# Relative-bias attention: the biased scores return to their PSUM bank, and ScalarE reads them there

## The chip, the cores and the metric

The kernel runs on one core of a Trainium2 chip. The metric is the device time of one execution in microseconds (us). TensorE multiplies and transposes (PE in the profile, its weight loads PEld), VectorE (DVE) and ScalarE (ACT) work element by element, GpSimd (POOL) does a little of the same, and SyncE (SP) issues the DMAs. Each engine runs its own instructions in order; between engines the program synchronises by semaphores, `wait_ge` and `then_inc`.

## The reference

The program computes a sequence model of four layers, each an attention-like part and a feed-forward part, on 8 sequences of 512 tokens and 128 features. Only the attention of the second layer (L1) is touched. In the reference:

```
q = shape(hidden_states @ Wq)          # H = 16 heads of DK = 64
k = shape(hidden_states @ Wk)
v = shape(hidden_states @ Wv)
scores = jnp.einsum('bhqd,bhkd->bhqk', q, k)
position_bias = compute_bias(s, s, rel_bias_table)   # depends on key - query only
scores = scores + position_bias
attn = jax.nn.softmax(scores, axis=-1)
out = jnp.einsum('bhqk,bhkd->bhqd', attn, v)
out = jnp.transpose(out, (0, 2, 1, 3)).reshape(b, s, H * DK)
return out @ Wo
```

So for every sequence and head a 512 x 512 matrix of scores gets a bias, a softmax along its rows, and is multiplied with the values. All of it is float32.

## The kernel before

The sequences pass one after the other through the same chain of stages. A hardware loop (`Fori`) takes the first six, and two more copies of the code, with the prefixes y and z in the tile names, take the last two; the stage therefore runs 8 times. The stage in question is `attn1`. It stands between the mixture-of-experts stage `moe` and the stage `lora1`, with nothing else beside it: all engines leave one stage before the next begins.

**Units and slots.** In the stage the work is cut into 64 units. A unit is 128 query rows of one head against all 512 keys, a tile of 128 x 512. Two heads go together (a head pair, eight units: four row blocks j, and in each the heads a = 0 and 1). All engines run through the same numbered slots, s = 0, 1, 2, ..., one unit a slot, each with its own lag written into the code. The letters below are those that the prediction uses for the steps of unit u:

- **S**: TensorE computes the scores of units s and s+1, two matmuls (line 2043), at every even slot s. They go to PSUM banks s % 4 and (s+1) % 4: `NS_ = 4` banks go round. From slot 4 on S has to wait until its two banks are free.
- **R**: VectorE adds the bias to the scores, takes the row's negated maximum `nmax`, and writes the sum to the SBUF tile `biased` (line 2145, one `tensor_tensor_reduce`; `maxed` counts it). Its slot is the unit's own.
- **E**: ScalarE takes exp(biased - max) into `prob`, with the row's sum in `den` (line 2116, followed by an instruction that reads the accumulator; `exped` counts it). It stands at slot u + 2 in ScalarE's order (`EXP = 2`).
- **V**: VectorE takes the reciprocal of `den` and scales `prob` by it (lines 2150 and 2152, `scaled`), at slot u + 1 of its own order, after R of unit u + 1.
- **T**: TensorE transposes the unit's `prob` (line 2050) at slot u + 4 (`TURN = 4`), into one of two banks that the ring of T and M shares, PS[4] and PS[7].
- **C**: ScalarE copies the transposed tile to `probt` (line 2124), also at slot u + 4, after that slot's E. It frees the ring's bank (`freed`).
- **W**: TensorE multiplies transposed probabilities and values (line 2064), at odd slots, for the head pair before.
- **M**: TensorE makes q, k and the values of the next head pair (lines 2014 and 2018), at slots 0, 2 and 4 of eight, between T of the even slot and T of the odd one. ScalarE moves each to SBUF (lines 2098 and 2095), after C of that even slot. At slot 4 of eight ScalarE also empties the product bank PS[5] (line 2105), and at slot 6 TensorE projects instead of making (line 2025).

So TensorE's order from an even slot s on is S(s, s+1), T(s-4), M, T(s-3), W. ScalarE's is E(s-2), C(s-4), the move of M, E(s-1), C(s-3). At the start of the stage C, T and W have nothing to do yet: TensorE's order is S(0,1), M, S(2,3), M, S(4,5), T(0), M, T(1), S(6,7), T(2), T(3), S(8,9), ..., with the first W at slot 13.

Of the kernel before, what the change touches and what calls it, by code (L numbers as in the profile page):

```python
# [19 lines left out]
ACT = mybir.ActivationFunctionType  # L20
# [4 lines left out]
P = 128  # L25
D = 128
SEQ = 512
NJ = SEQ // P
BIG = 3.0e38
# [42 lines left out]
def bass_mk_seq(nc, x, cols_f, cols_b, ends, wf, wb, lora, lora_cols, onehot, table, w2, out):  # L72
# [31 lines left out]
    PS = [BANKS[:, i, :] for i in range(8)]  # L104
# [1725 lines left out]
    def layers(b, scan_next, pre_next):  # L1830
# [113 lines left out]
        with Stage("attn1") as st:  # L1944
            def await_weights(sp):
# [14 lines left out]
            NS_, NP_, NT_ = 4, 6, 2 * PAIR  # L1960
# [1 line left out]
            qk = st.sb("qk", [P, 2, 2, SEQ])  # L1962
            vals = st.sb("vals", [P, 2, NJ, 2 * DK])
            toep = st.sb("toep", [P, 4, TW])
            biased = st.sb("biased", [P, NS_, SEQ])
            prob = st.sb("prob", [P, NP_, SEQ])
            probt = st.sb("probt", [P, NT_, SEQ])
            nmax, den, rden = (st.sb(n, [P, U]) for n in ("nmax", "den", "rden"))
            ot = st.sb("ot", [P, 2, SEQ])
            toep_ld = [st.sem(f"toep_ld{i}") for i in range(4)]  # L1970
            filled, freed, scored, maxed, exped, inverted, scaled = (
                st.sem(n) for n in ("filled", "freed", "scored", "maxed", "exped", "inverted", "scaled"))
# [21 lines left out]
            with nc.Block() as block:  # L1994
# [10 lines left out]
                def _(pe):  # L2005
# [26 lines left out]
                    for s in range(LAST):  # L2032
                        r, at = s // PAIR, s % PAIR
                        if s < U and s % 2 == 0:
                            j = unit(s)[1]
                            if at == 0:
                                pe.wait_ge(freed, place["make", r, 1] + 1)
                            if s >= NS_:
                                pe.wait_ge(maxed, s - NS_ + 2)
                            for a in range(2):  # L2040
                                o = DK * a
                                q, k = qk[o:o + DK, r % 2, 0, :], qk[o:o + DK, r % 2, 1, :]
                                nc.tensor.matmul(PS[(s + a) % NS_], q[:, j * P:(j + 1) * P], k,
                                                 start=True, stop=True).then_inc(scored, 1)
                        u = s - TURN
                        if 0 <= u < U:
                            pe.wait_ge(scaled, u + 1)
                            bank = ring(place["turn", u])
                            for kt in range(NJ):
                                last = nc.tensor.transpose(bank[:, kt * P:(kt + 1) * P],  # L2050
                                                           prob[:, u % NP_, kt * P:(kt + 1) * P], ident)
                            last.then_inc(filled, 1)
                        kt = WEIGH_AT.get(at)
                        w = r - (2 if at < TURN else 1)
                        if kt is not None and 0 <= w < NPAIR:
                            if kt == 0:
                                pe.wait_ge(freed, place["turn", PAIR * w + PAIR - 1] + 1)
                                pe.wait_ge(freed, place["make", w, 2] + 1)
                                if w:
                                    pe.wait_ge(emptied, w)  # L2060
                            for a in range(2):

                                first = PAIR * (w % 2) + a
                                last = nc.tensor.matmul(PS[5][DK * a:DK * (a + 1), :],
                                                        vals[:, w % 2, kt, DK * a:DK * (a + 1)],
                                                        probt[:, first:first + PAIR - 1:2, kt * P:(kt + 1) * P],
                                                        start=(kt == 0), stop=(kt == NJ - 1), skip_group_check=True)
                            if kt == NJ - 1:
                                last.then_inc(weighed, 1)
                        p = r - 2  # L2070
                        if at == PROJECT_AT and 0 <= p < NPAIR:
                            project(p)
                        if made_in(s):
                            make(*made_in(s))
# [11 lines left out]
                @block.scalar  # L2086
                def _(act):
                    def move(r, i):
                        n = place["make", r, i]
                        act.wait_ge(filled, n + 1)  # L2090
                        bank = RING[n % 2]
                        if i == 2:
                            if r >= 2:
                                act.wait_ge(weighed, r - 1)
                            nc.scalar.copy(vals[:, r % 2, :, :], bank.rearrange("p (j v) -> p j v", j=NJ)).then_inc(freed, 1)
                        else:
                            dst = qk[:, r % 2, i, :].rearrange("p (j t) -> p j t", j=NJ)
                            nc.scalar.copy(dst if i else dst[:, :, ::-1],
                                           bank.rearrange("p (j t) -> p j t", j=NJ)).then_inc(freed, 1)

                    def empty(w):
                        act.wait_ge(weighed, w + 1)
                        if w >= 2:
                            act.wait_ge(projected, w - 1)
                        nc.scalar.copy(ot[:, w % 2, :].rearrange("p (j t) -> p j t", j=NJ)[:, :, ::-1],
                                       PS[5].rearrange("p (j t) -> p j t", j=NJ)).then_inc(emptied, 1)

                    move(0, 0)
                    move(0, 1)
                    for s in range(LAST):  # L2110
                        e = s - EXP
                        if 0 <= e < U:
                            act.wait_ge(maxed, e + 1)
                            if e >= NP_:
                                act.wait_ge(filled, place["turn", e - NP_] + 1)
                            nc.scalar.activation(prob[:, e % NP_, :], biased[:, e % NS_, :], ACT.Exp, bias=nmax[:, e:e + 1],  # L2116
                                                 scale=-1.0, accum_out=den[:, e:e + 1]).then_inc(exped, 1)
                        u = s - TURN
                        if 0 <= u < U:
                            n = place["turn", u]  # L2120
                            act.wait_ge(filled, n + 1)
                            if u >= NT_:
                                act.wait_ge(weighed, (u - NT_) // PAIR + 1)
                            nc.scalar.copy(probt[:, u % NT_, :], RING[n % 2]).then_inc(freed, 1)  # L2124
                        w = s // PAIR - 2
                        if s % PAIR == EMPTY_AT and 0 <= w < NPAIR:
                            empty(w)
                        if made_in(s):
                            move(*made_in(s))
                    empty(NPAIR - 1)  # L2130

                @block.vector
                def _(dve):
                    V = nc.vector
                    for s in range(U + 1):
                        if s < U:
                            r, j, a = unit(s)
                            h = 2 * r + a
                            if j == 0:
                                dve.wait_ge(toep_ld[h % 4], 16 * (h // 4 + 1))  # L2140
                            dve.wait_ge(scored, s + 1)
                            if s >= NS_:
                                dve.wait_ge(exped, s - NS_ + 1)
                            c = P * (NJ - 1 - j)
                            V.tensor_tensor_reduce(biased[:, s % NS_, :], PS[s % NS_], toep[:, h % 4, c:c + SEQ], -1.0, BIG,  # L2145
                                                   ALU.add, ALU.min, nmax[:, s:s + 1]).then_inc(maxed, 1)
                        u = s - 1
                        if u >= 0:
                            dve.wait_ge(exped, u + 1)
                            V.reciprocal(rden[:, u:u + 1], den[:, u:u + 1]).then_inc(inverted, 1)  # L2150
                            dve.wait_ge(inverted, u + 1)
                            V.tensor_scalar(prob[:, u % NP_, :], prob[:, u % NP_, :], rden[:, u:u + 1], None,  # L2152
                                            ALU.mult).then_inc(scaled, 1)
                    dve.wait_ge(projected, NPAIR)
                    V.tensor_tensor(X[:, :, :], X[:, :, :], PS[6].rearrange(tiles, j=NJ), ALU.add)
# [211 lines left out]
```

## Time and profile before

| what | value |
|---|---|
| median of 3 runs | 5668.21 us (5660.7 to 5670.02) |
| the profiled execution | 5647.6 us, of which the span of the instructions is 5645.7 us |
| TensorE busy | 4758.2 us, 84% of the span |
| VectorE busy | 3632.7 us, 64% |
| ScalarE busy | 2719.9 us, 48% |
| line 2145 (R, in the six loop passes) | 384 times, mean 684 ns |
| line 2116 (E, in the six loop passes) | 384 times, mean 730 ns |

The profile is of one execution, so durations are compared with its own 5645.7 us; the difference of 20.6 us between its 5647.6 us and the median is how executions differ. A line of the profile that groups instructions gives the line of the kernel, the engine, the operation, the tile written and the tiles read, the shapes, the count, the busy time, the mean duration, and the idle time of the engine before them with what ended it. A timeline gives start, duration and the same names. Times of matmuls overlap in it: the end of a matmul is later than the moment at which the next one may enter, so intervals on TensorE are best read from start to start.

### The profile page before, as it was taken

The numbers are of one execution on the slowest core, as the hardware profiler recorded it, in microseconds if no ns is written. First come the engines' busy times: TensorE is split into PE (matmuls) and PEld (weight loads), VectorE is DVE, ScalarE is ACT, GpSimd is POOL, SyncE is SP. The second block draws the span as 40 slices with busy tenths as digits, with TensorE's granted clock in tenths as the row PEclk, the third lists the DMA queues.
The fourth block names the chain that finished last, engine by engine and source line by source line (L and its number), as shares of the span: only waits on it lengthen the run. The fifth ranks groups of instructions, "written<-read, shape, count | busy, mean of one in ns | idle before, by whom it ended". The sixth has DMA issues, their size and how long they took to land. (4 is left out here: it accounts for less than half of the span.)

```text
span 5645.7 us, 70330 instructions
## 1 busy us (share of the span) xinstructions
PE 4758.2 (84%) x22340; PEld 2223.0 (39%) x22340; DVE 3632.7 (64%) x8308; ACT 2719.9 (48%) x5086; POOL 1504.1 (27%) x1900
## 2 busy tenths in 40 slices
PE   4688887988879888898888988889887988889888
PEld 2244244432444324443244432444334543344344
DVE  5766855677556785657755677655865668556545
ACT  2255553644536454364542654435554455436443
POOL 2612620136200451106401064010630116201100
PEclk8899998998989999999899998999988999989889
DMA  4411310123101231012200132001320113201000
GB/s 134 134 40 57 107 63 2 47 67 100 53 3 53 73 100 40 3 53 94 86 33 16 40 111 82 20 23 48 107 75 16 35 46 107 74 5 53 1 27 6
DMA packets 150414, 315.66 MB, mean 56 GB/s; under 512 B 16192, under 2 KB 24896, under 8 KB 150000
## 3 DMA queue, kind: packets, MB, share of 16 engines
q1 hardware_dynamic: 150016, 310.82, 17.3%
q8 instruction: 193, 3.16, 0.2%
q14 instruction: 205, 1.68, 0.1%
HBM read 307.55 MB, written 3.21 MB: 55 GB/s over the span
## 5 line engine op out<-in xcount | busy, mean ns | idle before, releaser
L195 PE MATMUL BANKS<-WB 128*128 128x512 bf16 x2080 | 580.7, 431 | 252.0 <-DVE heads_parts_q L1327 65.4
L757 POOL TENSOR_TENSOR heads_work<-heads_work,heads_c_all 128x512 f32<-128x512 f32 x384 | 493.0, 1286 | 468.7 <-DVE heads_work L791 463.5
L1497 ACT ACTIVATE heads_prob<-BANKS 128x512 f32<-128x512 f32 (+3 forms) x768 | 376.7, 517 | 254.8 <-PE BANKS L1394 248.8
L211 POOL TENSOR_TENSOR rstd<-rstd,WF 128x4 f32<-128x4 f32 x24 | 24.2, 1006 | 1663.0 <-DVE rstd L229 1663.0
L724 PE MATMUL BANKS<-heads_work,WF 128*128 128x512 f32 x768 | 444.0, 663 | 7.0 <-DVE m_du L767 7.0
L195 PEld LDWEIGHTS BANKS<-WB 128*128 128x128 bf16 x2080 | 216.0, 108 | 586.6 <-issue 253.2
L1538 DVE TENSOR_REDUCE heads_nmax<-BANKS 128x1 f32<-128x512 f32 x384 | 248.7, 681 | 66.4 <-PE BANKS L1394 65.8
L404 POOL TENSOR_TENSOR rstd<-rstd,WF 128x4 f32<-128x4 f32 x48 | 48.5, 1010 | 908.6 <-DVE rstd L425 908.6
L2145 DVE CUSTOM_DVE_ANT_0 attn_biased<-BANKS,attn_toep 128x512 f32<-128x512 f32 x384 | 262.8, 684 | 34.1 <-DMA attn_toep<-bias_line 21.0
L2124 ACT COPY attn_probt<-BANKS 128x512 f32<-128x512 f32 x384 | 223.5, 582 | 126.6 <-PE BANKS L2050 124.1
L2116 ACT ACTIVATE attn_prob<-attn_biased,attn_nmax 128x512 f32<-128x512 f32 x384 | 280.3, 730 | 1.1 <-DVE attn_nmax L2145 1.0
L1394 PE MATMUL BANKS<-heads_parts_kT,heads_parts_qT 64*128 64x512 bf16 (+3 forms) x768 | 238.6, 368 | 46.1 <-DVE heads_nmax L1538 28.4
L1535 DVE CUSTOM_DVE_ANT_0 BANKS<-BANKS,WF 128x384 f32<-128x384 f32 (+3 forms) x512 | 242.0, 503 | 48.7 <-PE BANKS L1394 45.9
L869 PEld LDWEIGHTS BANKS<-last_x_w,last_x_a 128*128 128x128 f32 x1536 | 208.0, 200 | 165.7 <-ACT last_x_a L909 84.9
L782 DVE TENSOR_TENSOR BANKS<-BANKS,m_du 128x512 f32<-128x512 f32 x256 | 179.0, 699 | 139.6 <-PE BANKS L716 139.4
L869 PE MATMUL BANKS<-last_x_w,last_x_a 128*128 128x128 f32 x1536 | 215.8, 286 | 61.2 <-ACT last_x_a L909 61.2
L791 DVE TENSOR_TENSOR_SCAN heads_work<-BANKS,heads_work 128x512 f32<-128x512 f32 x192 | 233.3, 1215 | 41.0 <-POOL heads_work L753 40.4
L753 POOL TENSOR_TENSOR heads_work<-heads_b_all,m_du 128x512 f32<-128x512 f32 x192 | 251.5, 1310 | 0.2 <-DMA heads_b_all<-bc_rows 0.2
L2050 PEld LDWEIGHTS BANKS<-WF,attn_prob 128*128 128x128 f32 x1536 | 163.8, 140 | 209.1 <-DVE attn_prob L2152 134.7
L2050 PE MATMUL BANKS<-WF,attn_prob 128*128 128x128 f32 x1536 | 240.3, 281 | 6.7 <-ACT attn_probt L2124 3.7
L741 ACT ACTIVATE BANKS<-m_delta,WF 128x512 f32<-128x512 f32 x256 | 177.6, 694 | 131.9 <-DVE s_work L791 87.1
L1394 PE MATMUL BANKS<-heads_qm,heads_parts_kT 64*128 64x512 bf16 (+3 forms) x768 | 215.1, 355 | 21.9 <-DVE heads_nmax L1538 18.0
(919 smaller groups left out, 10554.0 us busy)
## 6 DMA issues: line engine op xcount, KB each, us to landing
heads_c_all<-bc_rows SPq DMA_DIRECT2D x384, 256.0 KB, 3.2
heads_b_all<-bc_rows SPq DMA_DIRECT2D x192, 256.0 KB, 3.6
attn_toep<-bias_line SPq DMA_DIRECT2D x96, 448.0 KB, 4.4
last_x_w<-in_w SPq DMA_DIRECT2D x48, 512.0 KB, 3.5
s_c_all<-bc_rows SPq DMA_DIRECT2D x64, 256.0 KB, 3.3
yheads_c_all<-bc_rows SPq DMA_DIRECT2D x64, 256.0 KB, 3.2
s_b_all<-bc_rows SPq DMA_DIRECT2D x32, 256.0 KB, 3.7
yheads_b_all<-bc_rows SPq DMA_DIRECT2D x32, 256.0 KB, 3.6
```

Of the source, the lines that this page charges most:

```text
L195: nc.tensor.matmul(bank, ident_b, bc(ident_b[:, 0:1], [P, SEQ]), start=True, stop=True)
L724: nc.tensor.matmul(SUM, ident, work[:, m % RW, :], start=(n == 0), stop=(n == NS - 1)).then_inc(acc, 1)
L753: nc.gpsimd.tensor_tensor(work[:, s % RW, :], b_all[:, k % RB, :], du[:, d, t, :], ALU.mult).then_inc(drv[1], 1)
L757: nc.gpsimd.tensor_tensor(work[:, m % RW, :], work[:, m % RW, :], c_all[:, m % RC, :], ALU.mult).then_inc(rd, 1)
L869: last = nc.tensor.matmul(DOWN[e % 2][:, j * D:(j + 1) * D], a1[:, i % 3, j * P:(j + 1) * P], down_part(i), start=(t == 0 and j == 0), sto ...
L1394: nc.tensor.matmul(take(kind, i)[:, lo:hi], left[rows, P * tile:P * (tile + 1)], right[rows, lo:hi], start=True, stop=True).then_inc(sem, 1)
L1497: nc.scalar.activation(prob[:, i % PR, lo:hi], bank("T", i)[:, lo:hi], ACT.Exp).then_inc(exped, 1)
L1535: V.tensor_tensor_reduce(got, got, W("early")[:, SEQ - hi:], -1.0, BIG, ALU.add, ALU.min, nmax[:, j, h:h + 1]).then_inc(maxed, 1)
L1538: V.tensor_reduce(nmax[:, j, h:h + 1], got, AX.X, ALU.max, negate=True).then_inc(maxed, 1)
L2050: last = nc.tensor.transpose(bank[:, kt * P:(kt + 1) * P], prob[:, u % NP_, kt * P:(kt + 1) * P], ident)
L2116: nc.scalar.activation(prob[:, e % NP_, :], biased[:, e % NS_, :], ACT.Exp, bias=nmax[:, e:e + 1], scale=-1.0, accum_out=den[:, e:e + 1]). ...
L2145: V.tensor_tensor_reduce(biased[:, s % NS_, :], PS[s % NS_], toep[:, h % 4, c:c + SEQ], -1.0, BIG, ALU.add, ALU.min, nmax[:, s:s + 1]).the ...
```

## The change

VectorE's step R writes its sum back to the PSUM bank that it read, not to the SBUF tile `biased`, which is gone. ScalarE's step E reads that bank. The bank is free for the next scores when E is done, so TensorE's step S now waits for `exped` with the same number with which it waited for `maxed`: before S(s, s+1) the E of units s-4 and s-3 has to be over, where it was the R of these units. VectorE's wait for E of unit s-4, which kept R from overwriting `biased`, is taken out. No instruction is added, dropped or put at another place of its engine's order.

```diff
@@ -1962,7 +1962,6 @@
             toep = st.sb("toep", [P, 4, TW])
-            biased = st.sb("biased", [P, NS_, SEQ])
             prob = st.sb("prob", [P, NP_, SEQ])
@@ -2036,7 +2035,7 @@
                             if s >= NS_:
-                                pe.wait_ge(maxed, s - NS_ + 2)
+                                pe.wait_ge(exped, s - NS_ + 2)
                             for a in range(2):
@@ -2113,7 +2112,7 @@
-                            nc.scalar.activation(prob[:, e % NP_, :], biased[:, e % NS_, :], ACT.Exp, bias=nmax[:, e:e + 1],
+                            nc.scalar.activation(prob[:, e % NP_, :], PS[e % NS_], ACT.Exp, bias=nmax[:, e:e + 1],
                                                  scale=-1.0, accum_out=den[:, e:e + 1]).then_inc(exped, 1)
@@ -2139,10 +2138,8 @@
                             dve.wait_ge(scored, s + 1)
-                            if s >= NS_:
-                                dve.wait_ge(exped, s - NS_ + 1)
                             c = P * (NJ - 1 - j)
-                            V.tensor_tensor_reduce(biased[:, s % NS_, :], PS[s % NS_], toep[:, h % 4, c:c + SEQ], -1.0, BIG,
+                            V.tensor_tensor_reduce(PS[s % NS_], PS[s % NS_], toep[:, h % 4, c:c + SEQ], -1.0, BIG,
                                                    ALU.add, ALU.min, nmax[:, s:s + 1]).then_inc(maxed, 1)
```

## Rows read from the trace of the kernel before

**Rows 1.** Busy time by engine, one stretch (start:end, length, busy, PEclk, DMA):
```profile
353.00:480.00 127.00, 124.83 (x643) 59.73 (x641) 79.19 (x257) 97.54 (x224) 0.00 (x0) 1.00 0.18 59
```
**Rows 2.** Line 2116: count, ns min/median/max, first and last start, forms:
```profile
L2116 ACT ACTIVATE attn_prob<-attn_biased,attn_nmax x384: 721/726/751, 360.6 to 3905.9; 128x512 f32<-128x512 f32 x192
...
L2116 ACT ACTIVATE zattn_prob<-zattn_biased,zattn_nmax x64: 721/726/751, 5128.5 to 5244.6; 128x512 f32<-128x512 f32 x64
```
**Rows 3.** Timeline, one pair of slots in mid-stage (start, duration, instruction, [idle before]):
```profile
400.75 1.13 PE L2043 MATMUL BANKS<-attn_qk 64*128 64x512 f32 x4
...
401.25 0.68 DVE L2145 CUSTOM_DVE_ANT_0 attn_biased<-BANKS,attn_toep 128x512 f32<-128x512 f32 x1
...
401.81 0.66 PE L2050 MATMUL BANKS<-WF,attn_prob 128*128 128x128 f32 x4
...
402.31 1.02 PE L2014 MATMUL BANKS<-XT,WF 128*128 128x512 f32 x2
...
402.51 0.58 ACT L2124 COPY attn_probt<-BANKS 128x512 f32<-128x512 f32 x1 [0.71 <-PE BANKS L2050]
...
403.24 0.63 PE L2050 MATMUL BANKS<-WF,attn_prob 128*128 128x128 f32 x4
403.37 0.58 ACT L2098 COPY attn_qk<-BANKS 128x512 f32<-128x512 f32 x1 [0.28 <-PE BANKS L2014]
...
403.80 1.08 PE L2064 MATMUL BANKS<-attn_probt,attn_vals 128*64 128x512 f32 x4
403.85 0.72 ACT L2116 ACTIVATE attn_prob<-attn_biased,attn_nmax 128x512 f32<-128x512 f32 x1
```
**Rows 4.** Timeline, start of the stage:
```profile
355.85 0.59 ACT L2098 COPY attn_qk<-BANKS 128x512 f32<-128x512 f32 x1 [0.27 <-PE BANKS L2014]
...
356.49 1.13 PE L2043 MATMUL BANKS<-attn_qk 64*128 64x512 f32 x4 [0.68 <-ACT attn_qk L2098]
...
360.61 0.72 ACT L2116 ACTIVATE attn_prob<-attn_biased,attn_nmax 128x512 f32<-128x512 f32 x1
...
360.72 1.13 PE L2043 MATMUL BANKS<-attn_qk 64*128 64x512 f32 x4
361.24 0.19 ACT L2116 ACTIVATION_READ_ACCUMULATOR attn_prob<-attn_biased,attn_nmax 128x1 f32 x1
...
361.46 0.16 DVE L2150 RECIPROCAL attn_rden<-attn_den 128x1 f32<-128x1 f32 x1 [1.92 <-ACT attn_prob L2116]
...
361.80 0.72 ACT L2116 ACTIVATE attn_prob<-attn_biased,attn_nmax 128x512 f32<-128x512 f32 x1
...
362.20 0.66 PE L2050 MATMUL BANKS<-WF,attn_prob 128*128 128x128 f32 x4 [0.35 <-DVE attn_prob L2152]
```
**Rows 5.** Timeline of TensorE, S of slots 14 and 16:
```profile
377.47 1.13 PE L2043 MATMUL BANKS<-attn_qk 64*128 64x512 f32 x4
...
380.56 1.13 PE L2043 MATMUL BANKS<-attn_qk 64*128 64x512 f32 x4
```
**Rows 6.** Timeline, mid-stage, a slot where ScalarE also empties PS[5]:
```profile
407.04 0.59 ACT L2105 COPY attn_ot<-BANKS 128x512 f32<-128x512 f32 x1
...
407.99 0.74 ACT L2116 ACTIVATE attn_prob<-attn_biased,attn_nmax 128x512 f32<-128x512 f32 x1
...
408.86 1.13 PE L2043 MATMUL BANKS<-attn_qk 64*128 64x512 f32 x4
```
**Rows 7.** Groups by line and form (count | busy us, mean ns | idle before):
```profile
L1497 ACT ACTIVATE heads_prob<-BANKS 128x512 f32<-128x512 f32 x480 | 274.5, 596 | 174.2 <-PE BANKS L1394 170.9
...
L909 ACT ACTIVATE last_x_a<-BANKS,WF 128x512 f32<-128x512 f32 x192 | 128.9, 686 | 173.3 <-PE BANKS L881 172.2
...
L1535 DVE CUSTOM_DVE_ANT_0 BANKS<-BANKS,WF 128x512 f32<-128x512 f32 x16 | 10.8, 706 | 0.8 <-PE BANKS L1394 0.7
```
**Rows 8.** Timeline, start of the stage: C of unit 0, then T's weights:
```profile
363.50 0.56 ACT L2124 COPY attn_probt<-BANKS 128x512 f32<-128x512 f32 x1
...
364.18 0.42 PEld L2050 LDWEIGHTS BANKS<-WF,attn_prob 128*128 128x128 f32 x4 [0.63 <-issue]
```

## The prediction

> **What bounds the kernel now.** I read the page's busy shares first (TensorE 84%), but the change touches one stage only, so the next view is the busy time in that stage: of the 127 us from 353 to 480 TensorE works 124.83, ScalarE 97.54 and VectorE 79.19, at a granted clock of 1.00 [rows 1]. TensorE bounds it. The view of line 2116 gives the count: 384 and 64 exponentials, and 64 more in the y copy of the code, are 512 = 8 stages of 64 units [rows 2]. Whatever one stage loses or gains counts eight times, since nothing runs beside it.
>
> Then the timeline, to see what order the releases come in. In mid-stage TensorE never waits. Start to start, S takes 1.06 us (400.75 to 401.81), T 0.50, M 0.93, the second T 0.56 and W the rest [rows 3], and S comes back after 4.055 us on average (400.75 to 408.86 is two rounds) [rows 3, 6]. The bank that S waits for was released by R: the R that starts at 401.25 and takes 0.68 belongs to the banks of an S two rounds later, at 408.86, so that wait has over 6 us of room. This is the room that the change gives away.
>
> **The change part by part.**
>
> *E reads PSUM.* It takes 726 ns now, median, from SBUF with a bias per partition [rows 2]. No row shows exactly the new form. The nearest one is line 909, PSUM to SBUF, same shape, bias per partition: 686. The exponential of line 1497, also from PSUM, takes 596, but its bias is a constant [rows 7]. I take 686, 0.04 less than now, and keep 596 (0.13 less) and 726 (nothing less) as the ends. The Trainium skill (ScalarE: Activation LUTs, What ACT_TABLE_LOAD costs) says that each per-partition operand adds about 93 ns to an ACTIVATE. The gap between the two rows, 90 ns, agrees; going by 596 in spite of it would make the result 3.6 us a stage instead of 4.0. In mid-stage the 0.04 is worth nothing, because ScalarE waits for TensorE: C waits 0.71 for T and the move 0.28 for M [rows 3].
>
> *R writes PSUM.* Line 1535 is this instruction, in place in a bank: 706 against 680 [rows 3, 7]. VectorE's 79 of 127 us cover the 0.03, and R at 401.25 is over 1.9 us before the E that reads it at 403.85 [rows 1, 3]. Without that cover it would be 64 x 0.03 = 1.9 us a stage. I take 0, and the wait that is dropped on VectorE is worth 0 too, as R never came near it: it is for an E four units back.
>
> *S waits for E.* This is what counts. S(s, s+1) now needs E(s-3). The signal comes after the accumulator is read: E(0) starts at 360.61, its read ends at 361.43, and the reciprocal that needs it starts at 361.46 [rows 4]. So it is 0.82 after E's start, 0.78 with the shorter E. From ScalarE's signal to TensorE the row nearest in kind is S(0) itself: the copy ends at 356.44 and S starts at 356.49, 0.05 [rows 4]. A bank is released for S 0.83 us after the start of E. (Another such pair shows 0.12, from 364.06 to 364.18 [rows 8]; with that, and no shorter E, it would be 0.94.)
>
> Mid-stage, with M in the round, the new ring is: S, T after 1.06, M after 0.50, ScalarE's move 1.06 after M's start (402.31 to 403.37), E 0.48 later (403.37 to 403.85), release 0.83 later: 3.93 us [rows 3], against 4.055 of TensorE's own work. It does not bind, by 0.12. Where ScalarE also empties PS[5], E starts at 407.99 and S at 408.86, 0.87 later [rows 6], against 0.83 needed: room 0.04. Without M the ring is 1.06 + 0.70 (T to C) + 0.48 + 0.83 = 3.07, against 3.09 of TensorE's work (377.47 to 380.56) [rows 3, 5]. So in mid-stage all rings stay just inside.
>
> At the start they don't. There TensorE has less work in a round (no W before slot 13), and in the kernel before S used that to run ahead of E: S(4,5) starts at 360.72, beside E(0), before E(1) at 361.80 has begun [rows 4]. Now it needs E(1). Followed slot by slot, with E(1) 0.04 earlier:
> - S(4,5): 361.76 + 0.83 = 362.59, instead of 360.72 (+1.87). T(0), ready since 362.20 [rows 4], now stands in TensorE's order behind the waiting S and comes at 363.65, and with it M, C and the move.
> - S(6,7): this round has an M, 3.93: 366.52. S(8,9): no M, 3.07: 369.59. S(10,11): 3.93, 373.52. S(12,13): 3.93, 377.45. In each of these rounds TensorE's own work is 3.1 at most with M (4.055 less W's 1.0) and 2.1 without.
> - S(14,15): from slot 13 on W is there, so TensorE's 4.055 binds again, not 3.93: 381.50. S(16,17): 3.09: 384.59, instead of 380.56 [rows 5]: 4.03, of which I keep 4.0.
>
> From there on TensorE has the same back-to-back work as before, with no idle time in which the 4.0 us could be caught up. The sum is 8 x 4.0 = 32 us on the profiled span of 5645.7, or 0.57%. On the median of the runs shown, 5668.2, this gives 5700.
>
> The bounds with the release at other places: with E at 596 it is 0.09 earlier in five rings, 4.0 - 0.45 = 3.55 a stage, 28 us. With release at 0.94 the five first rings cost 0.55 more, the one at slot 16 another 0.09, the six emptying slots 0.07 each, and two late rounds without M 0.09 each: 5.2 a stage, 42 us.
>
> The Trainium skill (PSUM — Partial Sum Buffer, Summary: rules for kernel authors) has a rule that speaks against this change: evacuate promptly. Taken as a general price it would make every round longer; by the rows it has one only in the rounds up to slot 14. The mid-stage case is the second rival below.
>
> **The rivals.**
> 1. *The lead doesn't matter* (no measurable change, 5671). Before, TensorE also waited in the first slots, 0.35 us before T(0) for one [rows 4]. If only the first wait counted, and later idle time absorbed it, less than 0.4 us a stage would be left, 3 us. Against it: E comes after C and the move, these come after T and M, and T stands behind S. So the ring closes over every round, and does not dissolve after the first. 6%.
> 2. *The mid-stage binds as well* (5725). The rooms there are 0.12, 0.04 and 0.02. If the release is 0.17 later than I take it, because E reads a bank more slowly or the signal is slow, the rounds up to slot 16 cost 1.0 more, ten rounds with M 0.05 each, six emptying ones 0.13, two late ones 0.15: 4.0 + 2.6 = 6.6 a stage, 53 us; I call it 57 with a weight load that can no longer be ahead. For it: thin rooms. Against it: no slow read of a bank in the rows [rows 7]. 14%.
> 3. *The clock falls at the start* (5716). The first 20 us get some 4 us more idle time on TensorE. The granted clock is 1.00 over the stage now [rows 1]. If it went to its lower level once per stage, at 1.2 GHz, for the time of one ring, TensorE's part of that ring, 1.06 + 0.50 + about 0.4, would double: 2 us, 16 us in all. 10%. The Trainium skill (TensorE: Matmul & The Clock Gate, HAM oscillation) warns of waits that make the clock fall; no row of this stage shows it yet.
> 4. *Faster* (5655). ScalarE is the busy engine in the first slots. If S were never held, because E(s-3) is over by then, and E took 596, the first 12 units would each gain 0.13 there: 1.6 us a stage, 13 us. It decides from the point where E(1) ends before 360.72; by [rows 4] E(1) starts only at 361.80. 3%.
>
> **How the numbers follow.** The forecast, 5700, has 67%; its own range is 5691 to 5712, from 28 us and from 42 and with a few us of difference between executions. The rivals have 6, 14, 10 and 3%. Two times that differ by less than 0.2%, 11 us, can't be told apart here. Faster is rival 4, 3%. Within 0.2% are rival 1 and a little of the rest, 7%. Slower 90%. The range of 5685 to 5728 leaves out the cases with no loss and what is beyond the second rival.
>
> **What would show it.** In the profile after, S(4,5) starts about 6.1 us after S(0,1) (4.2 before) and after the second E has ended; idle time of TensorE before line 2042 (S) of about 1.9 us at first and 0.9 in the next rounds, ended by ScalarE's E; S(16,17) about 28.1 us after S(0,1), 24.07 before; E at 0.69 us, R at 0.71. From slot 16 on rounds of 4.05 us again. The forecast is wrong if those rounds are longer than 4.1 (then rival 2), if matmuls of the first slots get longer (rival 3), or if S(6,7) and later ones don't wait (rival 1).

## The result and the profile after

| | before | after |
|---|---|---|
| median | 5669.11 us (4 runs, 5660.7 to 5670.4) | 5708.52 us (4 runs, 5702.9 to 5719.5) |
| profiled span | 5645.7 us | 5717.5 us |
| one stage, S(0,1) to the last C | 123.04 to 123.06 us, all 8 | 127.25 us in 2, 128.87 us in 6 |
| the same, sum of 8 | 984.3 us | 1027.7 us |

The changed kernel is slower: ratio 1.0071, 95% interval 1.0057 to 1.0086, 39 us between the medians. The forecast was 5700, +32, with a range of 5685 to 5728. Under "stage" the table has the time from the start of S(0,1) to the end of the last C, in the profiled execution.

The lines are numbered anew in the changed kernel: S is line 2042, E 2115 and R 2142. First E in the six loop passes (count, ns min/median/max); then the groups of the first stage (count | busy us, mean ns | idle before), and for comparison S in the same stage of the kernel before:

```profile
L2115 ACT ACTIVATE attn_prob<-BANKS,attn_nmax x384: 687/695/732, 363.4 to 3952.9; 128x512 f32<-128x512 f32 x192
```
```profile
L2115 ACT ACTIVATE attn_prob<-BANKS,attn_nmax 128x512 f32<-128x512 f32 x64 | 45.0, 704 | 0.3 <-DVE attn_nmax L2142 0.3
L2142 DVE CUSTOM_DVE_ANT_0 BANKS<-BANKS,attn_toep 128x512 f32<-128x512 f32 x64 | 44.4, 694 | 5.7 <-PE BANKS L2042 5.3 <-DMA attn_toep<-bias_line 0.2
...
L2042 PE MATMUL BANKS<-attn_qk 64*128 64x512 f32 x128 | 37.1, 656 | 6.1 <-ACT attn_prob L2115 5.4 <-ACT attn_qk L2097 0.7
```
```profile
L2043 PE MATMUL BANKS<-attn_qk 64*128 64x512 f32 x128 | 36.1, 641 | 0.7 <-ACT attn_qk L2098 0.7
```

E takes 695 ns, median, where it took 726 [rows 2]; R takes 694, mean, where it took 684. These are close to the sizes expected (0.69 and 0.71 us). What the forecast left out is the instruction behind R that reads the accumulator: it takes 142 ns, mean, where it took 82, so R's step is 0.07 us longer in all. The line of S is the one to look for: TensorE stands idle before S, and E ends that idle time, 5.4 us in this stage. The kernel before had no such entry; its S had idle time before it only once, 0.7 us, until ScalarE had copied k.

The timeline of TensorE in the sixth pass shows the waits one by one. It is the answer to [rows 4] and [rows 5]; there S(4,5) came 4.23 us after S(0,1), and S(16,17) 24.07:

```profile
3828.45 1.13 PE L2042 MATMUL BANKS<-attn_qk 64*128 64x512 f32 x4 [0.68 <-ACT attn_qk L2097]
...
3834.56 1.13 PE L2042 MATMUL BANKS<-attn_qk 64*128 64x512 f32 x4 [1.81 <-ACT attn_prob L2115]
...
3838.52 1.13 PE L2042 MATMUL BANKS<-attn_qk 64*128 64x512 f32 x4 [0.86 <-ACT attn_prob L2115]
...
3841.68 1.13 PE L2042 MATMUL BANKS<-attn_qk 64*128 64x512 f32 x4 [1.01 <-ACT attn_prob L2115]
...
3845.62 1.13 PE L2042 MATMUL BANKS<-attn_qk 64*128 64x512 f32 x4 [0.82 <-ACT attn_prob L2115]
...
3849.55 1.13 PE L2042 MATMUL BANKS<-attn_qk 64*128 64x512 f32 x4 [0.82 <-ACT attn_prob L2115]
...
3853.61 1.13 PE L2042 MATMUL BANKS<-attn_qk 64*128 64x512 f32 x4
...
3856.77 1.13 PE L2042 MATMUL BANKS<-attn_qk 64*128 64x512 f32 x4
...
3860.82 1.13 PE L2042 MATMUL BANKS<-attn_qk 64*128 64x512 f32 x4
```

The S start 6.11, 10.07, 13.23, 17.17, 21.10, 25.16 and 28.32 us after the first. Five of them, S(4,5) to S(12,13), show idle time before them that E ended; from S(14,15) on none does. The round up to S(16,17) is 3.16 us, where TensorE's own work took 3.09 [rows 5], and behind it the rounds are 4.05 us again (3856.77 to 3860.82). S(16,17) is 28.32 - 24.07 = 4.25 us later than before, and the stage ends 4.2 us later. Nothing is caught up.

In six of the eight stages there is more. Here is the first of them, as TensorE's timeline and as busy time by engine (PE, PEld, DVE, ACT, POOL) with the granted clock, which is the 1.00 or 0.50 behind them. The last row is the same place in the sixth pass, where the clock stays up:

```profile
365.37 2.06 PE L2042 MATMUL BANKS<-attn_qk 64*128 64x512 f32 x4 [1.81 <-ACT attn_prob L2115]
...
370.96 1.13 PE L2042 MATMUL BANKS<-attn_qk 64*128 64x512 f32 x4 [0.92 <-ACT attn_prob L2115]
```
```profile
359.30:365.40 6.10, 4.29 (x14) 1.19 (x14) 2.68 (x7) 3.80 (x7) 0.00 (x0) 1.00 0.60 236
365.40:368.80 3.40, 3.40 (x11) 1.90 (x12) 2.58 (x10) 1.06 (x3) 0.00 (x0) 0.50 0.00 0
...
3834.60:3838.00 3.40, 3.06 (x20) 2.03 (x20) 2.47 (x10) 2.16 (x5) 0.00 (x0) 1.00 0.00 0
```

After the wait of 1.81 us the clock is at its lower level, 1.2 GHz, for the next 3.4 us; the four matmuls of S take 2.06 us rather than 1.13, and the next S comes 5.59 us later, not 3.96. That is 1.62 us for each of six stages (128.87 - 127.25). The other two stages have the same wait of 1.81 us and no fall, so the wait alone doesn't decide it. The Trainium skill (TensorE: Matmul & The Clock Gate, HAM oscillation) tells of waits that throw the clock back in every tile of a loop. This trace agrees in part: the clock falls behind a wait, but in six stages of eight and not in all.

Together: 8 x 4.21 + 6 x 1.62 = 43.4 us, which is 1027.7 - 984.3. The profiled span grew by more, 71.8 us. The other 28 us lie outside the stage, in an execution that was the slowest of its four and had a mean granted clock of 0.921 against 0.927. The clock may well be all of it: 0.079 x 5717.5 - 0.073 x 5645.7 = 40 us, of which the six falls in the stage are 6 x 3.4 x 0.5 = 10, and this estimate leaves 30. No run tells whether the change has a part in the clock outside the stage; the medians leave little room for one. The medians, 39 us apart, are the better measure of the change, and stage lengths, which repeat to 0.03 us, the best one of its mechanism.

### The profile page after: what moved, and what is told of

Same layout as the page of the kernel before. It is cut to its first block and busy times, and to the rows that moved or that the text cites. A ratio compares the mean times of both kernels' runs of the same rounds, so it can differ in the third digit from the quotient of the medians.

```text
span 5717.5 us, 69962 instructions
## 1 busy us (share of the span) xinstructions
PE 4784.9 (84%) x22340; PEld 2241.2 (39%) x22340; DVE 3655.3 (64%) x8308; ACT 2710.4 (47%) x5086; POOL 1503.3 (26%) x1900
## 3 DMA queue, kind: packets, MB, share of 16 engines
q8 instruction: 193, 3.16, 0.2%
## 5 line engine op out<-in xcount | busy, mean ns | idle before, releaser
L2142 DVE CUSTOM_DVE_ANT_0 BANKS<-BANKS,attn_toep 128x512 f32<-128x512 f32 x384 | 266.4, 694 | 35.6 <-PE BANKS L2042 24.8
L2115 ACT ACTIVATE attn_prob<-BANKS,attn_nmax 128x512 f32<-128x512 f32 x384 | 270.2, 704 | 1.6 <-DVE attn_nmax L2142 1.6
L2042 PE MATMUL BANKS<-attn_qk 64*128 64x512 f32 x768 | 219.8, 649 | 36.3 <-ACT attn_prob L2115 32.2
```

Of the source, the lines that this page charges most:

```text
L2115: nc.scalar.activation(prob[:, e % NP_, :], PS[e % NS_], ACT.Exp, bias=nmax[:, e:e + 1], scale=-1.0, accum_out=den[:, e:e + 1]).then_inc(e ...
L2142: V.tensor_tensor_reduce(PS[s % NS_], PS[s % NS_], toep[:, h % 4, c:c + SEQ], -1.0, BIG, ALU.add, ALU.min, nmax[:, s:s + 1]).then_inc(maxe ...
```

## The experiments

Each was timed in turns with the kernel before. A stage's length is from the start of S(0,1) to the end of the last C, as above, and the sum is that of all eight in the profiled execution, one for each kernel. The ratios are of whole executions. All results together:

| run | ratio to before, 95% | stage, us | sum minus before's 984.3 |
|---|---|---|---|
| changed kernel | 1.0071 (1.0057 to 1.0086) | 127.25 or 128.87 | +43.4 |
| wait_only | 1.0097 (1.0082 to 1.0113) | 127.66 or 129.27 | +41.8 |
| fill | 1.0066 (1.0052 to 1.0079) | 127.25 | +33.7 |
| hybrid | 0.9993 (0.9984 to 1.0003) | 123.01 | -0.3 |
| table_after | 1.0043 (1.0029 to 1.0057) | 126.80 | +30.1 |
| lag_after | 1.0015 (1.0005 to 1.0024) | 123.89 | +6.8 |
| lag_before | 1.0016 (1.0008 to 1.0025) | 124.00 | +7.7 |
| table_lag_after | 1.0002 (0.9993 to 1.0011) | 122.47 | -4.5 |
| table_lag_before | 1.0000 (0.9989 to 1.0010) | 122.59 | -3.6 |
| table_before | 0.9982 (0.9973 to 0.9990) | 122.27 | -6.2 |

### wait_only: is it the wait, or the PSUM bank?

```diff
# the kernel before
-                                pe.wait_ge(maxed, s - NS_ + 2)
+                                pe.wait_ge(exped, s - NS_ + 2)
```

> The kernel before with one edit: S waits for E (exped) as in the changed kernel, while R still writes the SBUF tile and E still reads it. Theory (the wait alone costs the time, through the ring S, T, M, move, E, S at the start): E keeps its 0.73 us, so S(4,5) comes 6.15 us after S(0,1), and a stage from S(0,1) to the last C takes 123.0 + 4.4 = 127.5 us where TensorE's clock stays up and about 129.1 where it falls after the first wait; the whole kernel is 35 to 48 us slower than before, at 5704 to 5717. Rival (the PSUM bank as R's target and E's source costs it, by contention with TensorE's writes or slower accesses): most of the 39 us goes, and the time is within 12 us of before.

Its timeline at the start of the first stage, and S(20,21) and S(22,23) of the same stage:

```profile
357.48 1.13 PE L2043 MATMUL BANKS<-attn_qk 64*128 64x512 f32 x4 [0.68 <-ACT attn_qk L2098]
...
362.79 0.72 ACT L2116 ACTIVATE attn_prob<-attn_biased,attn_nmax 128x512 f32<-128x512 f32 x1
...
363.65 1.13 PE L2043 MATMUL BANKS<-attn_qk 64*128 64x512 f32 x4 [1.87 <-ACT attn_prob L2116]
...
394.11 1.13 PE L2043 MATMUL BANKS<-attn_qk 64*128 64x512 f32 x4
...
398.19 1.13 PE L2043 MATMUL BANKS<-attn_qk 64*128 64x512 f32 x4
```

S(4,5) comes 6.17 us after S(0,1), and stages take 127.66 us, or 129.27 in the three where the clock fell. The wait alone gives the whole loss, without a byte more in PSUM. It even costs 0.41 us a stage more than the changed kernel, and its E is the longer one: 0.86 from E's start to S (362.79 to 363.65) where the changed kernel has 0.84 (364.53 to 365.37 in its first stage). About half of the 0.41 arises up to S(16,17), which comes 28.53 us after S(0,1) and not 28.32. The rest arises in mid-stage, in the rounds where ScalarE also empties PS[5]: the last two rows above are 4.08 us apart, where the changed kernel has 4.05. E takes 0.74 us in these rounds and S comes 0.89 us after its start; in the changed kernel these are 0.71 and 0.86. So the room of 0.04 us that the prediction gives these rounds was in truth close to nothing: E 0.03 us longer makes them 0.03 us longer. The rival falls. The whole kernel, at 51 us over before by its medians, is slower than its stages' 41.8 explain and than the 35 to 48 expected. No run explains that rest; the other executions may have had more than the three falls of the clock in the profiled one, and falls in all eight stages would add 5 x 1.6 = 8 us, an estimate.

### fill: is the second loss the clock?

```diff
# the changed kernel
+                            if s == NS_:
+                                idle_products(PS[6], 8)
                             if s >= NS_:
                                 pe.wait_ge(exped, s - NS_ + 2)
```

> The changed kernel with 8 idle products (bf16, into the unused bank PS[6]) ahead of the wait of S(4,5), where TensorE has 1.81 us idle. Theory (TensorE's clock falls to 1.2 GHz because of that idle time, and this costs 1.6 us in each stage where it falls, 6 of 8 in the profile): no fall of the clock behind S(4,5), every stage 127.25 us from S(0,1) to the last C, and 6 x 1.6 = 10 us less than the changed kernel's 5708, so about 5699. Rival (the longer matmuls there are not the clock but the bank's contention with R and E, or the clock falls for idle time ahead of the stage): no change, 5708, and S(4,5) still takes 2 us.

TensorE in the first stage, with the idle products (nothing reads their result) on line 195:

```profile
365.91 1.90 PE L195 MATMUL BANKS<-WB 128*128 128x512 bf16 x8
367.88 1.13 PE L2044 MATMUL BANKS<-attn_qk 64*128 64x512 f32 x4
```
```profile
367.00:372.00 5.00, 4.08 (x26) 2.43 (x26) 3.56 (x12) 3.66 (x10) 0.00 (x0) 1.00 0.00 0
```

All eight stages take 127.25 us, S(4,5) takes 1.13 us again and the granted clock stays at 1.00 behind it. S(4,5) still starts 6.11 us after S(0,1) (361.77), so the products cost nothing, and what goes is just the 6 x 1.62 = 9.7 us: the sum falls from +43.4 to +33.7. The same bank accesses are there, so it was not they that made matmuls long. The ratios (1.0066 and 1.0071) can't tell 0.17% apart with intervals of this width; the stage lengths do.

### hybrid: is the loss all before slot 16?

```diff
# the changed kernel
+            FIRST = 16
+            biased = st.sb("biased", [P, NS_, SEQ])
+            def summed(u):
+                return biased[:, u % NS_, :] if u < FIRST else PS[u % NS_]
...
-                                pe.wait_ge(exped, s - NS_ + 2)
+                                pe.wait_ge(maxed if s - NS_ < FIRST else exped, s - NS_ + 2)
...
# in words: E reads and R writes summed(u); for NS_ <= s < FIRST, VectorE's wait of before stands again
```

> The first 16 units of a stage go as in the kernel before (R into SBUF, S waits for R), the other 48 as in the changed kernel (R and E in the PSUM bank, S waits for E). Theory (all of the loss arises up to slot 16, and from there on the ring just fits into TensorE's own 4.05 us): as before, 5669 within 6 us, stages of 123.0 to 123.2 us. Rival (the rounds in mid-stage lose a little each, or PSUM accesses slow TensorE there): 48 of 64 units carry three quarters of the loss, at least 20 us over before.

The groups of its first stage, and S(16,17) and the round behind it on TensorE (S(0,1) was at 361.03):

```profile
L2121 ACT ACTIVATE attn_prob<-BANKS,attn_nmax 128x512 f32<-128x512 f32 x48 | 33.8, 705 | 0.0
L2150 DVE CUSTOM_DVE_ANT_0 BANKS<-BANKS,attn_toep 128x512 f32<-128x512 f32 x48 | 33.3, 694 | 0.9 <-PE BANKS L2048 0.9
```
```profile
385.11 1.13 PE L2048 MATMUL BANKS<-attn_qk 64*128 64x512 f32 x4
...
389.16 1.13 PE L2048 MATMUL BANKS<-attn_qk 64*128 64x512 f32 x4
```

48 of 64 units go through the bank, and the stage takes 123.01 us; before it was 123.04. S(16,17) comes 24.08 us after S(0,1), and the round behind it takes 4.05. In mid-stage the bank costs nothing, thin as the rooms are that the prediction gives. The rival needed 20 us; the interval ends at +0.03%.

### table_after: what holds E(1)?

```diff
# the changed kernel; early is a tile of one column
                     move(0, 0)
                     move(0, 1)
+                    nc.scalar.activation(early[:, :], W("minus_half")[:, 0:1], ACT.Exp)
```

> The changed kernel with a one-column Exp on ScalarE after the first two moves, where ScalarE is idle for 2.3 us, so that the table load of 1.28 us is over before E(0). Theory (S(4,5) hangs on E(1), E(1) on E(0), and E(0) on the table load): E(0) and all that follows come 1.3 us earlier, S(4,5) has 0.5 us of idle time before it rather than 1.8, the clock does not fall there; 8 x 1.3 + 6 x 1.6 = 20 us less than the changed kernel: 5688. Rival (E(0) is held by R(0) or the copy ahead of it as well): under 4 us of gain.

The table load is an instruction of ScalarE that the program doesn't write out. It stands once a stage, ahead of the first E, in the kernel before too (its trace, line 2116, all 8 of them):

```profile
L2116 ACT ACT_TABLE_LOAD  x8: 1283/1283/1283, 359.3 to 5127.2; - x8
```

The start of the first stage of table_after:

```profile
360.58 1.13 PE L2043 MATMUL BANKS<-attn_qk 64*128 64x512 f32 x4 [0.68 <-ACT attn_qk L2098]
...
363.28 0.69 ACT L2117 ACTIVATE attn_prob<-BANKS,attn_nmax 128x512 f32<-128x512 f32 x1
...
364.91 0.58 ACT L2098 COPY attn_qk<-BANKS 128x512 f32<-128x512 f32 x1 [0.85 <-PE BANKS L2014]
...
365.40 0.69 ACT L2117 ACTIVATE attn_prob<-BANKS,attn_nmax 128x512 f32<-128x512 f32 x1
...
366.23 1.13 PE L2043 MATMUL BANKS<-attn_qk 64*128 64x512 f32 x4 [1.36 <-ACT attn_prob L2117]
```

E(0) comes 1.42 us earlier (2.70 after S(0,1), not 4.12), as expected, but E(1) only 0.44 (4.82, not 5.26). Between them in ScalarE's order stands the move of k, and that waits 0.85 us for TensorE's M. So the expected 1.3 us a stage was wrong: 0.45 came. The clock did not fall in any stage, with 1.36 us of idle time instead of 1.81. Of the 43.4 us, 13.3 went, where 20 were expected. That the median, 5684.8, is near the 5688 expected is luck: in these turns the kernel before had a median of 5660.5, not 5669.1. This pointed to ScalarE's order, and to the next runs.

### lag_after and lag_before: E one slot earlier in ScalarE's order

```diff
# the changed kernel, and the kernel before
-            EXP, TURN = 2, 4
+            EXP, TURN = 1, 4
```

> The changed kernel with EXP = 1: in ScalarE's order E(u) stands one slot earlier, ahead of the C and the move of its slot's neighbour, and all else stays. Theory (the loss is the ring S, T, M, move, E, S, which exists because E(s-3) stands behind the move of slot s-2; not the wait for E as such): E(1) no longer waits for the move of k, S(4,5) comes about 5.6 us after S(0,1) rather than 6.11, and the later S are no longer held by ScalarE but by TensorE's own work; S(16,17) at 24.0 to 24.8, a stage 123 to 124 us, the clock stays up; whole kernel within 8 us of before. Rival (a bank that has to pass through both R and E is held too long with four banks, wherever E stands): stages stay above 126 us, at least 25 us over before.

> The kernel before with EXP = 1. It tells how much of what lag_after does would come without the change. Theory: T(0) is still held by E(0) behind the table load, so little changes at the start; the C of the first slots are held less, a stage takes 122.4 to 123.0 us, 0 to 5 us less than before in the whole. Rival (ScalarE's order already was the best for the kernel before): a stage gets longer than 123.04 us.

The start of the first stage of lag_after, and E(3) and T(1) in the first stage of lag_before:

```profile
359.34 1.13 PE L2042 MATMUL BANKS<-attn_qk 64*128 64x512 f32 x4 [0.68 <-ACT attn_qk L2097]
...
364.14 0.68 ACT L2115 ACTIVATE attn_prob<-BANKS,attn_nmax 128x512 f32<-128x512 f32 x1
...
364.96 1.13 PE L2042 MATMUL BANKS<-attn_qk 64*128 64x512 f32 x4 [1.32 <-ACT attn_prob L2115]
...
366.87 0.69 ACT L2115 ACTIVATE attn_prob<-BANKS,attn_nmax 128x512 f32<-128x512 f32 x1 [0.43 <-DVE attn_nmax L2142]
...
367.55 0.58 ACT L2123 COPY attn_probt<-BANKS 128x512 f32<-128x512 f32 x1
...
368.27 0.63 PE L2049 MATMUL BANKS<-WF,attn_prob 128*128 128x128 f32 x4 [0.70 <-ACT attn_probt L2123]
...
368.83 1.13 PE L2042 MATMUL BANKS<-attn_qk 64*128 64x512 f32 x4
```
```profile
363.25 0.72 ACT L2116 ACTIVATE attn_prob<-attn_biased,attn_nmax 128x512 f32<-128x512 f32 x1 [0.39 <-DVE attn_nmax L2145]
...
364.68 0.63 PE L2050 MATMUL BANKS<-WF,attn_prob 128*128 128x128 f32 x4 [1.61 <-ACT attn_probt L2124]
```

The same wait, with the same buffers, costs 0.85 us a stage (123.89 - 123.04) instead of 4.2 to 5.8. Only S(4,5) still waits for E; S(6,7) follows T without a gap. So it was not the wait for E as such but where E stood: behind C and the move, which wait for TensorE. The rival falls. The stage is in the range expected; S(16,17) comes 25.16 us after S(0,1), later than the 24.0 to 24.8 expected.

For the kernel before, my expectation was wrong and its rival right: 124.00 us, 0.96 more. Now C(0) stands behind E(3), which waits for VectorE, 0.43 us in lag_after and 0.39 in lag_before, and T(1) waits for C(0), 0.70 and 1.61 us. With EXP = 1 the changed kernel and the kernel before differ by 0.11 us a stage, and the changed one is the shorter.

### table_lag_after and table_lag_before: both edits, on the changed kernel and on the one before

> The changed kernel with both edits: the Exp table loaded early and EXP = 1. In table_after E(0) came at 2.70 us but E(1) only at 4.82, held by the move of k; with EXP = 1 nothing of that stands ahead of it. Theory: E(1) at about 3.5 us, S(4,5) at TensorE's own pace, 4.23 to 4.4 us, T(0) right behind it, S(16,17) at 23 us; a stage of 121.7 to 122.4 us, so 5 to 11 us less than the kernel before. Rival (the wait for E costs in the first rounds even so, over VectorE's R, V, R sequence): a stage of 123 us or more, no faster than before.

> The kernel before with both edits. Theory (with E early and in front, the wait for E costs nothing more, and the changed kernel and the one before are equal): the same stage as table_lag_after within 0.3 us, and the same time within 0.1%. Rival (releasing the bank at R still lets TensorE run ahead and is worth something): at least 0.5 us a stage less than table_lag_after.

TensorE's S in the first stage of table_lag_after, then of table_lag_before:

```profile
358.18 1.13 PE L2043 MATMUL BANKS<-attn_qk 64*128 64x512 f32 x4 [0.68 <-ACT attn_qk L2098]
...
362.45 1.13 PE L2043 MATMUL BANKS<-attn_qk 64*128 64x512 f32 x4
...
366.25 1.13 PE L2043 MATMUL BANKS<-attn_qk 64*128 64x512 f32 x4
```
```profile
353.61 1.13 PE L2044 MATMUL BANKS<-attn_qk 64*128 64x512 f32 x4 [0.68 <-ACT attn_qk L2099]
...
357.84 1.13 PE L2044 MATMUL BANKS<-attn_qk 64*128 64x512 f32 x4
...
361.68 1.13 PE L2044 MATMUL BANKS<-attn_qk 64*128 64x512 f32 x4
```

S(4,5) comes after 4.27 and 4.23 us, S(6,7) after 8.07 in both; stages take 122.47 and 122.59 us. With E early enough the change costs nothing, and the two ways are equal, to 0.12 us a stage in the changed kernel's favour. The 4.5 us that the stages of table_lag_after gained would be 0.08% of the whole; the whole kernel shows +0.02%, interval -0.07 to +0.11%, so the gain can't be told. It is less than the 5 to 11 us expected.

### table_before: a version that beats both

> The kernel before with the Exp table loaded early and EXP = 2 as it was. Theory (EXP = 1 cost the kernel before 0.96 us a stage, because C(0) then stands behind E(3), which waits for VectorE; the early table gave 1.4 us of that back and more): E(0) at 2.70 us, T(0) at 5.3 rather than 5.7, S(16,17) at 22.9 to 23.7, a stage of 121.9 to 122.7 us; 3 to 9 us less than before in the whole, at the edge of what can be told. Rival (the C of the first slots are held by the moves and not by E(0)): a stage of 123.0 us as before.

The edit is the added line of table_after, in the kernel before. The start of its first stage:

```profile
361.18 1.13 PE L2044 MATMUL BANKS<-attn_qk 64*128 64x512 f32 x4 [0.68 <-ACT attn_qk L2099]
...
363.88 0.72 ACT L2118 ACTIVATE attn_prob<-attn_biased,attn_nmax 128x512 f32<-128x512 f32 x1
...
365.41 1.13 PE L2044 MATMUL BANKS<-attn_qk 64*128 64x512 f32 x4
...
366.47 0.66 PE L2051 MATMUL BANKS<-WF,attn_prob 128*128 128x128 f32 x4
...
368.69 1.13 PE L2044 MATMUL BANKS<-attn_qk 64*128 64x512 f32 x4
```

With only the table loaded early, T(0) starts 5.29 us after S(0,1), right behind S(4,5), where it was 5.71 [rows 4]; S(6,7) comes after 7.51, where it was 8.28 (364.77 - 356.49 in the trace before). The stage takes 122.27 us, and the kernel 5652.0 against 5661.4: ratio 0.9982, 0.9973 to 0.9990. That is a small gain, but one clear of noise: it is faster than the kernel before, and so than the changed one.

## Why the prediction was right

**The count and the bound.** The loss came in all eight stages, and none of them caught it up. TensorE is back to back in mid-stage, and hybrid shows that the room given away there cost nothing.

**The first wait.** S(4,5) was forecast 6.10 us after S(0,1) (362.59 - 356.49) and came at 6.11.

**The ring.** Forecast rounds of 3.93, 3.07, 3.93, 3.93 and then 4.055; measured 3.96, 3.16, 3.94, 3.93 and 4.06. The chain of S, T, M, move, E and S holds, and lag_after shows the link that closes it: with E out from behind C and the move the ring is gone.

**The term that was mis-sized** is the release at the slots that begin a head pair, S(8,9) and S(16,17). The rounds that end with them took 3.16 us each, where I had 3.07 and 3.09. That is 0.16 of the 0.21 us by which a stage lost more than forecast, 4.21 and not 4.0; most of the rest is the round up to S(6,7), 3.96 for 3.93. Over eight stages the 0.21 is 1.7 us. The two E that release S(4,5) and S(8,9) of the timeline above are these:

```profile
3833.71 0.70 ACT L2115 ACTIVATE attn_prob<-BANKS,attn_nmax 128x512 f32<-128x512 f32 x1
...
3840.76 0.69 ACT L2115 ACTIVATE attn_prob<-BANKS,attn_nmax 128x512 f32<-128x512 f32 x1
```

From the end of E's ACTIVATE it is 0.15 us to S(4,5) (3834.41 to 3834.56) and 0.23 to S(8,9) (3841.45 to 3841.68). At the slots that begin a head pair the code has S wait for two semaphores, `freed` too. That this is the cause is argued from the code, not shown by a run; these are also the rounds without an M, and no run separates the two.

**The rival that came true beside the forecast** is the third, the fall of the clock. I gave it 10%, as a thing of all stages or none, with 2 us each. It came in 6 of 8, with 1.62 us each, 9.7 us. The prediction set against it that the granted clock was 1.00 over the stage; but in the kernel before that stage had no wait of 1.8 us on TensorE. By the prediction's own sign, longer matmuls in the first slots, this rival held in those six stages. The ring and this rival together are 33.7 + 9.7 = 43.4 us in the stages, and 39 between the medians. So the mechanism of the forecast gave 33.7 of it, close to its 32. That the whole, 5708.5, still lies inside the forecast's own range of 5691 to 5712 is partly luck, as this range was worked out without the clock.

**The other rivals.** The mid-stage did not bind (hybrid), though only just: with E 0.03 us longer some of its rounds did (wait_only). The lead did matter, as the loss is in every stage. Faster was out of reach: E took 695, not 596, and E(1) began at 5.26 us, a microsecond after S(4,5) could have.

**E's and R's durations** were off by 0.01 us (695 for 686, 694 for 706). The 0.03 us by which E became shorter was worth something, since wait_only, without it, loses 0.41 us a stage more; an error of 0.01 is then about 0.1 us a stage, an estimate in proportion. R's part was not tried alone. At the start of the sixth pass R ended one wait of E, 0.26 us before E(2), and S(6,7) waits for E(3), which stands behind the move.

## What to carry to other kernels

When a buffer's release is moved from one engine to another, don't only ask how much longer it is held in steady state. Write down what stands ahead of the new releaser in its engine's order; if that in turn waits for the engine that wants the buffer, a ring closes, and it shows where that engine has the least work of its own: here at the start of a stage, not in its middle. Before giving up the buffer scheme, try the releaser's place in its queue: one constant, EXP, took away five sixths of the stages' loss here (6.8 us left of 43.4). And when a change puts a new wait before TensorE, ask for its price twice, once for the wait and once for the clock behind it: here 1.81 us of wait were followed by another 1.62 in six stages of eight.

## What the runs showed of the hardware

- An idle time of 1.81 us on TensorE at this place was followed by the clock at 1.2 GHz in 6 of 8 stages, one of 1.87 us in wait_only in 3 of 8; 1.36 us (table_after) and 1.32 us (lag_after) never in 8. The longer wait had the fewer falls, so their number is not a fixed price of a wait, and one trace of each kernel doesn't show what decides it. Eight idle products in the gap kept the clock up in all 8 stages of fill, at no cost.
- The in-place reduction into a PSUM bank takes 10 ns more than into SBUF (694 and 684), and the accumulator read behind it 142 ns for 82. The exponential, with a bias per partition, takes 31 ns less from PSUM than from SBUF (695 and 726).
- The table load of 1.28 us on ScalarE fits into idle time when a one-column activation asks for it; the copies that follow did not cause another load (one load in the stage in table_after, table_before and both table_lag runs).
- Stage lengths repeat to a few hundredths of a microsecond between the passes of a kernel where the clock stays up (at most 0.07, in table_lag_after). Whole executions of the kernel before lay up to 0.35% from their median, and the granted clock differs with them: 5640.8 us at 0.929, 5673.5 at 0.921. Effects of 0.1% can be read from the former and not from the latter.
